# Row sums of the two longer query tiles on ScalarE, and a group's weighting moved into the next step, in a one-core attention and mixer program

## What is computed

```python
q = (x @ wq_w.T + wq_b).reshape(b, t, H, HD)
k = (x @ wk_w.T + wk_b).reshape(b, t, HKV, HD)
v = (x @ wv_w.T + wv_b).reshape(b, t, HKV, HD)
scores = jnp.einsum('bqhd,bkd->bhqk', q, k1) / jnp.sqrt(jnp.float32(HD))
scores = jnp.where(causal, scores, -jnp.inf)
weights = jax.nn.softmax(scores, axis=-1)
attn = jnp.einsum('bhqk,bkd->bqhd', weights, v1)
return attn.reshape(b, t, H * HD) @ wo_w.T + wo_b
```

## Time and profile before

| | us |
|---|---|
| runs of the kernel, median (lowest to highest of 3) | 3110.08 (3106.48 to 3111.67) |
| the profiled execution, its own time | 3110.4 |
| its span from first to last instruction | 3108.7 |
| mean granted TensorE clock over the span | 0.954 |
| busy: PE / PEld / DVE / ACT / POOL | 2869.6 / 2139.2 / 1697.3 / 837.6 / 879.2 |
| first and last transpose of the maxima (L664, 64 of them) | at 67.3 and 1687.7 |

### The profile page before, as it was taken

The page is one execution under the profiler, slowest core; times in us unless marked ns, Lnnn a source line. Parts: engine busy times, 40 slices in busy tenths (PEclk is TensorE's granted clock), DMA queues, the critical chain, the costliest instruction groups (busy, mean ns, idle before and its releaser), DMA issues. The chain is left out here.

```text
span 3108.7 us, 41774 instructions
## 1 busy us (share of the span) xinstructions
PE 2869.6 (92%) x16704; PEld 2139.2 (69%) x16704; DVE 1697.3 (55%) x2976; ACT 837.6 (27%) x1485; POOL 879.2 (28%) x1379
## 2 busy tenths in 40 slices
PE   5889999999999999999998786999999999999988
PEld 4556767667676676676775545877777777777766
DVE  4564464553644545636444144666666666666654
ACT  2342242231422322314223012222222222222220
POOL 0112122121221221212212014434353535353521
PEclk9889999999999999999998868999999999999989
DMA  5665445444445554445354330010101010102011
GB/s 150 173 174 153 156 102 159 106 113 141 111 92 159 113 147 120 102 140 121 81 145 117 100 138 1 1 35 21 38 18 41 14 48 8 54 1 55 1 28 28
DMA packets 103619, 272.29 MB, mean 88 GB/s; under 512 B 12122, under 2 KB 23514, under 8 KB 101122
## 3 DMA queue, kind: packets, MB, share of 16 engines
q1 hardware_dynamic: 99488, 268.56, 31.8%
q10 hardware_dynamic: 3938, 1.06, 0.2%
HBM read 168.40 MB, written 50.33 MB: 70 GB/s over the span
## 5 line engine op out<-in xcount | busy, mean ns | idle before, releaser
L483 DVE TENSOR_REDUCE top<-ps_attn 128x1 f32<-128x512 f32 (+3 forms) x704 | 420.0, 619 | 353.1 <-PE ps_attn L648 353.0
L394 ACT ACTIVATE pt<-ps_attn 128x512 f32<-128x512 f32 (+1 forms) x704 | 382.6, 559 | 758.6 <-PE ps_attn L675 756.1
L1379 PE MATMUL ps_mixer<-m_w_hi,m_xt_hi 128*128 128x512 f32 x1024 | 416.3, 407 | 0.0
L334 POOL TENSOR_SCALAR_AFFINE_SELECT pt<-pt 128x512 f32<-128x512 f32 x256 | 166.5, 662 | 875.6 <-ACT pt L394 873.2
L1380 PE MATMUL ps_mixer<-m_w_hi,m_xt_lo 128*128 128x512 f32 x1024 | 401.7, 392 | 0.0
L1381 PE MATMUL ps_mixer<-m_w_lo,m_xt_hi 128*128 128x512 f32 x1024 | 401.4, 392 | 0.0
L645 PE MATMUL ps_attn<-k_stack,q_stack 96*128 96x512 f32 (+3 forms) x1024 | 310.1, 360 | 55.1 <-DVE top L483 48.6
L675 PE MATMUL ps_attn<-q_stack,k_stack 97*128 97x512 f32 (+3 forms) x1024 | 285.4, 338 | 9.6 <-DMA q_stack<-top_rows 8.5
L645 PEld LDWEIGHTS ps_attn<-k_stack,q_stack 96*128 96x128 f32 x1024 | 178.7, 193 | 147.7 <-DVE top L483 114.6
L1045 ACT CAST m_xt_hi<-ps_mixer 128x512 fp32r<-128x512 f32 x192 | 104.4, 589 | 629.5 <-PE ps_mixer L1374 629.2
L492 DVE RECIPROCAL att<-ps_attn 128x128 f32<-128x128 f32 x256 | 241.1, 944 | 18.1 <-PE ps_attn L683 18.1
(11 more groups left out here) (207 smaller groups left out, 4992.5 us busy)
## 6 DMA issues: line engine op xcount, KB each, us to landing
xr<-in_a_x SPq DMA_DIRECT2D x64, 512.0 KB, 7.0
q_stack<-q_hi SPq DMA_DIRECT2D x128, 256.0 KB, 5.6
wq_hi<-wq_split SPq DMA_DIRECT2D x56, 512.0 KB, 4.1
wq_lo<-wq_split SPq DMA_DIRECT2D x56, 512.0 KB, 5.2
q_stack<-q_lo SPq DMA_DIRECT2D x64, 256.0 KB, 6.8
wo_hi<-wo_split SPq DMA_DIRECT2D x8, 2048.0 KB, 8.9
wo_lo<-wo_split SPq DMA_DIRECT2D x8, 2048.0 KB, 13.2
x<-xr SPq DMA_DIRECT2D x32, 512.0 KB, 2.8
```

Source lines behind the costliest of these rows:

```text
L394: nc.scalar.activation(pt[k][:, heads[0]:heads[0] + len(heads), :].rearrange("p j t -> p (j t)"), ps[:, ST0 + n % 2, 0:width * len(heads)] ...
L483: nc.vector.tensor_reduce(out, ps[:, S0 + n % 2, 0:width * len(heads)].rearrange("p (j k) -> p j k", k=width), AX.X, ALU.max).then_inc(s_u ...
L1379: nc.tensor.matmul(out, a_hi, b_hi, start=first, stop=False)
```

## The change

ACT now sums the softmax row of query tiles 2 and 3 itself. After DVE has found the extreme of a unit (the key scale is negated, so it is a minimum now), ACT reads the same PSUM bank once more, takes exp of the difference and lets the instruction's accumulator give the row sum (`row_sum`, L423 of the new file). This is done for the first 8 of the 11 units. The bank becomes free only then: `scores` of units 2 to 9 wait for ACT's sum, not for DVE's reduction. DVE inverts all 8 sums at once (`den_invert`), POOL spreads each over 32 columns (`spread`), and PE transposes the result into the upper half of bank DEN. The ones product in `weigh` covers only columns 0 to 255. DVE's four reciprocals of DEN become two, and one copy of the 256 transposed columns (`take_inverse`).

The weighting of a group is now wholly in the following step, in three places: k=0 after `scores` unit 0, k=1 after unit 5 of the scores, k=2 and 3 with the transposes after unit 6. `invert`, `divide` and `finish_high` move from the middle of the step to its end; projection chunks stand closer together early in the step; `output` waits for the last group only ahead of its eighth chunk.

```diff
+    SUMMED, SUM_TILES = 8, 2
+    SUM_COL = (T // P - SUM_TILES) * P
...
+                def spread(G):
+                    pool.wait_ge(den_inv_done, G + 1)
...
+                    nc.gpsimd.tensor_copy(att[:, G % 2, SUM_COL:T].rearrange("p (i j d) -> p (i j) d", j=GH, d=HEAD),
...
+                def row_sum(G, u):
...
+                    act.wait_ge(s_used, n + 1)
...
+                    nc.scalar.activation(spent[:, 0:width], ps[:, S0 + n % 2, 0:width], ACT.Exp, scale=-1.0,
+                                         bias=top[:, j * TILES + i:j * TILES + i + 1].bitcast(F32),
+                                         accum_out=den[:, i - (TILES - SUM_TILES), j:j + 1]).then_inc(den_done, 1)
...
+                    for u in range(U):
                         if inside(M):
+                            exps(M, (u,))
+                        if inside(M + 1):
+                            row_sum(M + 1, u + 2)
+                        if u == 1 and (G := wq_group(M)) is not None:
                             wq_high(G)
+                        if u == 2 and inside(M + 2):
+                            q_high(M + 2)
...
                     for G in finishes(M):
                         finish_high(G)
...
                     if n >= 2:
-                        pe.wait_ge(s_used, n - 1)
+                        held = S_UNITS[(n - 2) % U][0] >= TILES - SUM_TILES
+                        if held:
+                            pe.wait_ge(den_done, (n - 2) // U * SUMMED + (n - 2) % U + 1)
+                        else:
+                            pe.wait_ge(s_used, n - 1)
...
+                def weigh(G, k):
+                    for bank, side, end in ((AV, v_sb[:, (G // GROUPS) % 2, k, :], T), (DEN, ones[:, :], SUM_COL)):
...
                 def weigh_rest(G):
                     pe.wait_ge(sel_done, TILES * (G + 1))
+                    for k in range(2, TILES):
+                        weigh(G, k)
+                    pe.wait_ge(den_rep_done, G + 1)
+                    for i in range(TILES - SUM_TILES, TILES):
+                        mm = nc.tensor.transpose(ps[:, DEN, i * P:(i + 1) * P], att[:, G % 2, i * P:(i + 1) * P], ident_f)
...
+                    if inside(M + 1):
+                        scores(M + 1, 0)
                     if second is not None:
                         transposes(second, 2)
                     if inside(M - 1):
+                        weigh_first(M - 1)
+                    if project:
+                        q_part(M + 2, (1,))
+                    if inside(M + 1):
+                        scores(M + 1, 1)
...
                     if second is not None:
                         transposes(second, 3)
...
+                        if project and u < 3:
+                            q_part(M + 2, ((3,), (4, 5), (6, 7))[u])
...
+                        if u == 3 and inside(M - 1):
+                            weigh_second(M - 1)
+                        if u == 4 and inside(M - 1):
+                            weigh_rest(M - 1)
```

More of the change, by code:

```diff
@@ L356, in _ @@
                     if inside(M):
-                        cut(M, 0)
+                        for k in range(TILES):
+                            cut(M, k)
                     for G in finishes(M):
@@ L360, in _ @@
                     if inside(M):
-                        for k in range(1, TILES):
-                            cut(M, k)
+                        spread(M)
                     if M % GROUPS == GROUPS - 1 and inside(M):
@@ L539, in _ @@
                     tiles = [(coming(M, 2 + t), t) for t in range(TILES) if coming(M, 2 + t)]
-                    for b, t in tiles:
-                        moments(dve, b, t)
+                    if inside(M + 1):
+                        tops(M + 1, (0, 1))
                     if second is not None:
@@ L544, in _ @@
                         x_low(second, 3)
[L545 to L560 removed]
+                    for b, t in tiles:
+                        moments(dve, b, t)
+                    if inside(M + 1):
+                        tops(M + 1, (2, 3))
+                    for b, t in tiles:
+                        normalise(dve, b, t)
+                    if (G := wq_group(M)) is not None:
+                        wq_low(G)
+                    if inside(M + 1):
+                        tops(M + 1, (4,))
                     if inside(M + 2):
@@ L677, in turned_scores @@
                     mm.then_inc(st_ready, 1)
-                def weigh(G, blocks, last):
-                    for k in blocks:
-                        for bank, side in ((AV, v_sb[:, (G // GROUPS) % 2, k, :]), (DEN, ones[:, :])):
-                            for j in range(GH):
-                                mm = nc.tensor.matmul(ps[j * HEAD:(j + 1) * HEAD, bank, k * P:T], side, pt[k][:, j, :],
-                                                      start=(k == 0), stop=(k == TILES - 1))
-                    mm.then_inc(last, 1)
+                def weigh(G, k):
+                    for bank, side, end in ((AV, v_sb[:, (G // GROUPS) % 2, k, :], T), (DEN, ones[:, :], SUM_COL)):
+                        for j in range(GH) if end > k * P else ():
+                            mm = nc.tensor.matmul(ps[j * HEAD:(j + 1) * HEAD, bank, k * P:end], side, pt[k][:, j, 0:end - k * P],
+                                                  start=(k == 0), stop=(k == TILES - 1 or bank == DEN and end - k * P == P))
+                    return mm
                 def weigh_first(G):
@@ L715, in output @@
                         for c in range(CH):
+                            if run == 0 and t == 0 and c == CH - 1:
+                                pe.wait_ge(olo_done, GROUPS * (b + 1))
                             mm = split_product(ps[:, (PROJ, MISC)[t % 2], :], at_hi[:, c, tok], at_lo[:, c, tok], w_hi[:, c, :],
```

141 lines of the change are left out of this document (76 added, 65 removed).

## The result

| | before | after |
|---|---|---|
| runs, median (lowest to highest of 4) | 3108.28 (3106.39 to 3111.67) | 3167.0 (3163.28 to 3169.01) |
| span of the profiled execution | 3108.7 | 3166.2 |
| mean granted TensorE clock | 0.954 | 0.936 |
| first, 8th, 32nd and last transpose of the maxima at | 67.3, 251.6, 877.2, 1687.7 | 74.8, 270.3, 926.3, 1760.7 |

What follows compares the result with a forecast made beforehand. PE was taken to bound the attention at clock 1.00. Six full batch entries -18.3, last -1, first +3, end -5 and clock +7.5 gave -13.8, from 3110.4 to 3096.6, so 3097 us; range 3068 to 3140.

Steps and rivals of the forecast that it cites:

- Plain steps: Steps without input work: 17.95 us, PE waiting 0.6 for ACT before unit 9 and 0.4 for DVE before unit 10.
- The stack of q: Third copy lands at T+18.3 at most, next unit 0 wants it at 17.8: 0.2 us wait, 0 to 0.6.
- The sum: One row sum on ACT: 0.68 us for 512 keys and 0.60 for 384.
- rival B: ACT's exp and sum chain binds if a sum exceeds 0.80 us; T moves by 0.45: 3115 us, chance 0.18.
- M%8 = 5 and 6: Input steps: 21.5 us where it was 22.4, and 29.1 for 27.97 with 2.9 idle ahead of tile 3's transposes.
- The clock: One fall to 1.2 GHz, 1.6 us, in each of 7 batch entries: 11.2 less about 4, entered as +7.5.
- Rival C: Falls behind both idle times of M%8 = 5 and 6, each 3.3 us longer at half speed: 3132 us, chance 0.13.
- A: No wait for the stack of q (-7), none or few clock falls (-8): 3080 us, chance 0.12.
- D: Clock falls once in each of 35 plain steps, at 1.6 us, from PE's short waits: 3153 us, chance 0.10.
- the late pieces: The stack of q and the maxima's row, both arriving late around the start of the next step.
- The first batch entry: Less cover for the maxima's row, weight splitting already making PE wait: +3 us, between -5 and +12.
- The end of the attention: PE's 6.24 us wait for the last at_lo covered by seven output chunks, two reciprocals less ahead: -5 us.

Runs made afterwards that it cites:

- e1: The changed kernel with DVE's `den_invert` moved to the end of the step, behind `x_low` and `kv_in`: 3108.84 us.
- e10: e4 with POOL's `spread` at the head of its step, and the group M%8 = 2 finishes late finished at that step's head: 3064.02 us.
- e4: The changed kernel with `den_invert` last, `q_high` later, and `x_high` and `x_low` of tile 2 ahead of unit 1's sum and reduction: 3073.55 us.
- e9: The changed kernel with POOL's `spread` at the head of its step, ahead of the cuts, except in M%8 = 2: 3108.5 us.
- e2: The changed kernel with `q_high` behind exps unit 4 instead of 2 in M%8 = 6, and `q_low` one reduction later: 3155.94 us.
- e7: e4 with each sum on ACT made twice, the second counting as the bank's release: 3405.92 us.

## Why the prediction was wrong

**Plain steps: right in the mean, partly by luck.** 17.95 was forecast for each; 17.25, 18.60, 17.91 and, where nothing is late ahead of it (e1), 17.25 were measured, 17.75 in the mean. The wait of unit 9 for ACT is there (0.52 us in M=26, for 0.6), the wait of unit 10 for DVE is not. The stack of q is waited for 0.44 and 0.33 us in M=27 and M=28, inside the range of 0 to 0.6, and not in M=26. Against what did not come stands a wait that was not forecast: the 18.60 of M%8 = 3 has the wait of `den_inv` again, 3.17 us at the head of the step, with 0.43 us for PE behind it; e10 takes both away.

**The sum: right in length, wrong in form.** By shape, in the stretch of the earlier trace rows:

```profile
L423 ACT ACTIVATE spent<-ps_attn,top 128x512 f32<-128x512 f32 x232 | 159.6, 688 | 220.3 <-DVE top L510 217.5
...
L423 ACT ACTIVATE spent<-ps_attn,top 128x384 f32<-128x384 f32 x232 | 134.9, 582 | 72.9 <-DVE top L510 72.9
...
L423 ACT ACTIVATION_READ_ACCUMULATOR spent<-ps_attn,top 128x1 f32 x464 | 91.1, 196 | 0.0
```

688 and 582 ns stand where 680 and 600 were taken; a second instruction of 196 ns, not foreseen, overlaps the first by 0.1 us, so the sum holds a bank for 0.78 us at 512 keys, just under the 0.80 from which rival B was to decide. The Trainium skill ("ScalarE: Activation LUTs", section "What ACT_TABLE_LOAD costs") gives 280 ns and 0.833 ns a column for an activation whose bias is a pointer. By that rule the two are estimated at 706 and 600; the trace agrees to 3%.

**M%8 = 5 and 6: the step that failed.** The working was "x_low of tile 1 now comes after the division" and 21.5 us. It named what stands behind the division and left out the instruction between: `den_invert`, whose wait for `spread` reaches back over POOL and ACT to that same division. Without the wait that number holds: e1, e4 and e9 measured 21.2 to 21.3 in M=29. (The chain as added up there is 8.0 us; from the T+13.7 of the plain step that is 21.7, not 21.5.) For M%8 = 6 it put 29.1, with the wait of 2.9 us for tile 2 (2.88 measured); the terms given there make 28.9. It had neither the 4.3 us of `den_inv` ahead of `kv_in` nor the 5.2 us at ACT's head that `q_high` brings. e4, with all three gone, takes 28.4. The wait of `den_inv` alone (58 us by e1 and e9) is as large as the measured loss, and with that of `q_high` (11 us by e2) it is about the 70 us by which the forecast missed. That the kernel stands at the time of before without it is a balance: what PE gained and what the other two waits cost happen to be alike. With all three gone it is 34 us faster than before, for the 13 forecast, and it then has no wait for tile 2 either, which the forecast had counted.

**The clock: right in kind, too small.** One fall of 1.6 us a batch entry was counted (the term of +7.5 in the sum is 7.2 by its own figures, 11.2 less 4). M=30 lost 0.14 of 38.4 us, 5.4 us of full-speed work, and M=31 another 0.09 of 18.8, 1.7 us. Rival C had this mechanism in this place, with the clock below 1 for more than 5 us in each M%8 = 6, and its condition was met: five of the seven stretches above are at 0.50, and every step M%8 = 6 has a mean of 0.85 or 0.86. But it knew nothing of the waits that bring the falls; its 3132 is 35 us short, and no row shows its 3.3 us for a fall. That the clock fell here and not in the M=30 of before, with its 1.7 us idle, fits the longer idle times, but no run varied the idle time alone, and e4 has a step with 2.83 us of idle ahead of it and no fall.

**Rivals A, B and D.** Plain steps at 1.00 rule out D: PE is busy there for 16.7 of 17.25 us. By what the Trainium skill reports ("TensorE: Matmul & The Clock Gate", section "A second HAM failure mode: psum-queue depth-cycling") they would have alternated; the trace does not agree. Of B's waits for ACT only that of unit 9 is there, and T did not move by it. Under e7's doubled sum it does. A was half right: the late pieces are mostly hidden, which e4 shows, while the clock did not hold.

**The first batch entry and the ends.** +3 was put for the first, within -5 to +12; +18.7 came, 9.8 of it in M=6, by the waits above, and 7.5 ahead of the first transpose. PE waits there for a sum, the sum for DVE's reduction, and this stands behind `wq_low`, which waits for ACT's `wq_high`, now behind the sum of unit 3. PE, and below the dots DVE and ACT:

```profile
64.42 0.44 PE L694 MATMUL ps_attn<-k_stack,q_stack 96*128 96x384 f32 x1 [3.30 <-ACT spent L423]
...
61.28 1.91 DVE L562 TENSOR_TENSOR wq_lo<-wq_raw,wq_hi 128x1024 fp32r<-128x1024 f32 x1 [2.80 <-ACT wq_hi L453]
...
59.20 2.06 ACT L453 CAST wq_hi<-wq_raw 128x1024 fp32r<-128x1024 f32 x1
```

Two more waits of 2.03 and 2.57 us follow. The prediction looked at PE's waits for DVE in this stretch and not at what now stands ahead of the weight splitting on ACT. e4 and e10 keep 7.2 and 8.0 us of it; no run tried another order there. One more step was missed: in M=8, where 0.3 us less was forecast, PE waits 10.10 us for the stack of q, for 5.45 before, and the step takes 52.05 us for 48.20. It takes 50.0 to 53.2 in every experiment, and no run looked for the cause. The end of the attention gained 12.3 us, not 5: the first output product comes 17.2 us after the last transpose, where it came 28.35 after it, and no wait stands ahead of it:

```profile
1777.84 0.47 PE L625 MATMUL ps_attn<-wo_hi,at_hi 128*128 128x512 f32 x1
```

The mixer's -3.2 us is not explained.

## What to carry to other kernels

When work moves between engines, list every instruction that gains a wait, however short, and follow that wait back over the queues of all engines: where it reaches an instruction late in the step, everything behind the waiting one on its queue is late too. Reuse of a single buffer is such a wait, and moving either end of it (the consumer earlier, or the writer to where nothing urgent follows) was worth more here (58 us) than the moved work itself (e4 is 34 us faster than the kernel before). Cost the steps that are unlike the others one by one, since the plain ones were right here and two steps in eight decided the sign.

## What the runs showed of the hardware

- An activation with an accumulator output is two instructions on ScalarE: the activation, and one of 196 ns that reads the accumulator, with some 0.1 us of overlap.
- TensorE's granted clock was 0.50, its level of 1.2 GHz, for some 4 us of full work behind 5.4 us of idle time and for some 6 us behind a further 2.9. In e4 it fell behind 2.84 us of idle time in M=30 and not behind 2.83 in M=46. 16.7 busy of 17.25 us, and no wait over 0.53 us, did not lower it in M=26, nor did the like in M=27 and M=28.
- A unit passes here through TensorE, VectorE and ScalarE over two banks. 6.0 us more of ScalarE's work a step made the step 6.5 us longer, with ScalarE 74% busy and TensorE's mean clock at 0.87 instead of 1.00.
